# One block for all stages of a two-layer hybrid kernel, and one normalisation in the place of two

## What is computed

```
for stage in (selective scan, mixture, multi-query attention, mixture,
              grouped-query attention, capacity mixture, windowed attention, capacity mixture):
    x = x + stage(layernorm(x))        # layernorm: (x - mean) / sqrt(var + 1e-5)
```

```
xn = layernorm(x)
mu = jnp.mean(xn); var = jnp.var(xn)
xn = (xn - mu) * rsqrt(var + EPS) * gamma
```

## Time and profile before

| | us |
|---|---|
| median of 3 runs | 1926.79 (1923.84 to 1929.45) |
| the profiled execution | 1924.93 |
| its span, first to last instruction | 1923.1 |
| mean granted TensorE clock | 0.944 of full speed |

### The profile page before, as it was taken

The page is one execution under the profiler, slowest core; times in us unless marked ns, Lnnn a source line. Parts: engine busy times, 40 slices in busy tenths (PEclk is TensorE's granted clock), DMA queues, the critical chain, the costliest instruction groups (busy, mean ns, idle before and its releaser), DMA issues. The chain is left out here.

```text
span 1923.1 us, 35959 instructions
## 1 busy us (share of the span) xinstructions
PE 1702.3 (89%) x10911; PEld 1365.3 (71%) x10912; DVE 1355.2 (70%) x2857; ACT 1002.8 (52%) x2208; POOL 664.6 (35%) x640
## 2 busy tenths in 40 slices
PE   3877999599999899979999997987799999988986
PEld 1224888477777788857777796765688888887764
DVE  7997666878885566678777748554888888657643
ACT  4654443477874344357777633111687887633111
POOL 1663222266662022236656503000455555212000
PEclk8997999799999899989999997999899999988988
DMA  0000110100000011010000003696211000021984
GB/s 29 0 1 27 45 48 28 53 20 19 19 8 1 23 50 49 27 55 23 25 19 14 1 1 120 202 252 178 75 31 30 25 30 11 1 84 55 262 239 134
DMA packets 39478, 111.15 MB, mean 58 GB/s; under 512 B 5504, under 2 KB 23664, under 8 KB 32240
## 3 DMA queue, kind: packets, MB, share of 16 engines
q1 hardware_dynamic: 39408, 110.26, 19.8%
HBM read 109.19 MB, written 1.05 MB: 57 GB/s over the span
## 5 line engine op out<-in xcount | busy, mean ns | idle before, releaser
L1320 POOL TENSOR_TENSOR xn<-xn 128x512 f32<-128x512 f32 x138 | 180.2, 1306 | 272.0 <-DVE xn L1215 272.0
L1306 POOL TENSOR_SCALAR prob<-prob,recip 128x256 f32<-128x256 f32 (+2 forms) x256 | 229.8, 912 | 71.6 <-DVE recip L1199 71.5
L1110 ACT ACTIVATE prob<-banks,peak 128x256 f32<-128x256 f32 (+3 forms) x384 | 190.4, 501 | 104.1 <-DVE peak L1190 97.9
L959 PE MATMUL banks<-pt,v 128*128 128x256 f32 (+3 forms) x768 | 204.4, 409 | 6.9 <-ACT pt L1045 6.9
L959 PEld LDWEIGHTS banks<-pt,v 128*128 128x128 f32 x768 | 145.2, 190 | 73.9 <-issue 31.9
L914 PE MATMUL banks<-k_hi,q_hi 128*128 128x256 f32 (+2 forms) x384 | 154.2, 401 | 25.1 <-DVE k_lo L1206 24.8
L1190 DVE TENSOR_REDUCE peak<-banks 128x1 f32<-128x256 f32 (+3 forms) x384 | 161.6, 448 | 20.5 <-PE banks L918 17.6
L594 POOL TENSOR_TENSOR gu_lo<-gu,gu_hi 128x512 fp32r<-128x512 f32 x36 | 46.8, 1301 | 294.6 <-ACT gu_hi L552 294.6
L935 PE MATMUL banks<-ident,prob 128*128 128x128 f32 x864 | 142.5, 282 | 3.2 <-DVE pt L1043 3.2
L563 ACT ACTIVATE silu<-gate 128x512 f32<-128x512 f32 x72 | 43.1, 599 | 159.1 <-PE up L515 159.0
L1215 DVE TENSOR_TENSOR xn<-xn,ropes 128x512 f32<-128x512 f32 x138 | 124.3, 901 | 0.0
(11 more groups left out here) (249 smaller groups left out, 5193.3 us busy)
## 6 DMA issues: line engine op xcount, KB each, us to landing
wgu<-in_w_gu SPq DMA_DIRECT2D x32, 1408.0 KB, 14.8
wd<-in_w_d SPq DMA_DIRECT2D x32, 704.0 KB
gu<-in_w SPq DMA_DIRECT2D x36, 256.0 KB, 2.7
wd<-in_w SPq DMA_DIRECT2D x36, 128.0 KB, 2.0
wkv<-in_mha_kv SPq DMA_DIRECT2D x16, 256.0 KB, 2.6
wq<-in_mqa_q SPq DMA_DIRECT2D x16, 128.0 KB, 2.0
wo<-in_mqa_o SPq DMA_DIRECT2D x16, 128.0 KB, 2.2
wq<-in_gqa_q SPq DMA_DIRECT2D x16, 128.0 KB, 2.1
```

The costliest lines, as they stand in the source:

```text
L959: last = pe.matmul(o_bank[:, x * P:to], v[:, s, x, at:at + P], pt[:, s, x, first:first + to - x * P], start=(j == 0), stop=(j == NQ - 1))
L1110: last = act.activation(prob[:, s, cols[t]:cols[t] + n], s_bank[gi][:, psum_col[t]:psum_col[t] + n], ACT.Exp, bias=peak[:, s, t:t + 1], ac ...
L1306: last = pool.tensor_scalar(part, part, recip[:, s, t:t + 1], None, ALU.mult)
L1320: pool.tensor_tensor(cosed[:, r % 2, :], cosed[:, r % 2, :], swap[:, r % 2, :], ALU.add) \
```

## The change

All stages come to stand in one block; the barriers, and the separate blocks at the start and the end, go. A stage becomes an object that holds a body for each engine, and each engine's program in the one block runs the bodies one after the other. SBUF is cut into four fixed zones (0 to 64, 64 to 96, 96 to 142 KB, and the rest) in place of allocation per stage, and every tile is put into a zone such that what the next stage loads early does not overlap what is still in use. PSUM is one tensor of 8 banks, used by each stage as before.

The links between stages are these. VectorE's statistics of tile pair j wait for the addition to that pair, by a count that the additions raise:

```
-        for r in range(self.rounds):
-            src = g.xn if r else g.x
-            for h in range(2):
...
+        for t in range(NT):
+            if t % 2 == 0 and self.after:
+                count, first = self.after
+                wait(dve, count, first + t // 2 + 1)
+            dve.bn_stats(g.bn[:, t, :], g.x[:, t, :]).then_inc(self.stats.sem, 1)
```

```
+            if self.again:
+                op = act.activation(g.std[:, cut], g.mv[:, cut, 1], ACT.Sqrt, scale=1.0 + EPS, bias=g.eps2[:, 0:1])
+            else:
+                op = act.activation(g.std[:, cut], g.mv[:, cut, 1], ACT.Sqrt, bias=g.eps[:, 0:1])
```

with eps2 = EPS * EPS: normalising twice divides by sqrt(var + EPS) * sqrt(var / (var + EPS) + EPS), which is sqrt(var * (1 + EPS) + EPS * EPS). The store is cut into four in the last stage:

```
+        if out is not None:
+            for t in range(0, NT, 2):
+                sp.wait_ge(c["added"].sem, t // 2 + 1)
+                sp.dma_start(out[:, t:t + 2, :], g.x[:, t:t + 2, :]).then_inc(c["stored"].sem, 16)
+            sp.wait_ge(c["stored"].sem, 16 * NT // 2)
```

More of the change, by code:

```diff
@@ L1 @@
-from contextlib import ExitStack
+import math
 import concourse.bass as bass
@@ L438, in selective_scan @@
-    finish(nc, [*c.values(), *norm.counts])
-def mixture(nc, g, d):
-    c = {n: Count(nc, n, p) for n, p in (
+    _, _, early, _ = st.areas()
+    late = Area(st.nc, g.zones[0][0], g.zones[1][1])
+    xw = late.take("xw", [P, NC, XROWS], F32)
+    dtw = late.take("dtw", [XROWS, H], F32)
+    vecs = late.take("vecs", [P, 2 * NC + NC * N_STATE], F32)
+    pick1 = late.take("pick1", [A3, HALF], F32)
+    pick = late.take("pick", [A3, HALF, P], BF16)
+    rows = late.take("rows", [XROWS, T], F32)
@@ new lines, in selective_scan @@
+    rest = early.take("rest", [A3, T], F32)
+    part = early.take("part", [A3, T], BF16)
+    stack = late.take("stack", [A3, T], BF16)
+    nega = late.take("nega", [P, NC, N_STATE], F32)
+    size = early.take("size", [P, NC, T], F32)
+    e = early.take("e", [P, NC, T], F32)
+    lg = early.take("lg", [P, NC, T], F32)
+    relu = early.take("relu", [P, NC, T], F32)
+    lost = early.take("lost", [P, NC, T], F32)
+    delta = late.take("delta", [P, NC, T], F32)
+    du = late.take("du", [P, NC, T], F32)
@@ L448, in mixture @@
+def mixture(st, g, d, free, after):
+    c = st.c = {n: st.count(n, p) for n, p in (
         ("loaded", 0), ("gu_even", 0), ("gu_odd", 0), ("d_even", 0), ("d_odd", 0), ("logits", 0), ("gates", 0),
@@ L695, in attention @@
+def attention(st, g, d, after, name, kv_every, window, gamma=None, again=False):
     UNITS = HEADS * NSEQ
@@ new lines, in out_half @@
+        def out_half(u):
+            t, half = u // 2, u % 2
+            wait(pe, c["wo_low"], HEADS)
+            wait(pe, c["o_low"], u + 1)
+            to = banks[:, t // 2, (t % 2) * H:(t % 2 + 1) * H]
+            for h in range(WO):
+                o_hi, o_lo = (part[:, half, h, :] for part in o_stage)
+                hi, lo = (w[:, half * WO + h, :] for w in (wo_hi, wo_lo))
+                pe.matmul(to, o_hi, hi, start=(half == h == 0), stop=False)
+                pe.matmul(to, o_hi, lo, start=False, stop=False)
+                last = pe.matmul(to, o_lo, hi, start=False, stop=(half == 1 and h == WO - 1))
+            last.then_inc(c["o_used"].sem, 1)
@@ L1359, in capacity_mixture @@
+def capacity_mixture(st, g, d, free, after, opened, out=None):
+    c = st.c = {n: st.count(n, p) for n, p in (
         ("loaded", 0), ("own_v", 0), ("logits", 0), ("shared_w", 0), ("peak", 0), ("expd", 0), ("masked", 0),
@@ L1876, in stages @@
-def stages(nc, g, ins):
-    selective_scan(nc, g, ins)
-    mixture(nc, g, ins)
-    attention(nc, g, ins, "mqa", kv_every=HEADS, window=False, gamma=g.gamma, again=True)
-    mixture(nc, g, ins)
-    attention(nc, g, ins, "gqa", kv_every=4, window=False)
-    capacity_mixture(nc, g, ins)
-    attention(nc, g, ins, "mha", kv_every=1, window=True)
-    capacity_mixture(nc, g, ins)
+    low, high = -(-nc.sbuf_base // 64) * 64, nc.sbuf_usable_end // 32 * 32
+    kept = Area(nc, low, high)
+    g.x = kept.take("x", [P, NT, H], F32)
```

2905 lines of the change are left out of this document (1476 added, 1429 removed).

## The result

The new kernel takes 1896.91 us (median of four runs, 1892.51 to 1902.75) where the kernel before took 1927.11 in the same comparison: a ratio of 0.9846, 95% interval 0.9812 to 0.988. The new kernel is 30 us faster; 11.8 were forecast, and 1896.9 lies outside the range of 1904 to 1921.5. The profiled execution took 1892.51 (span 1890.7) against 1924.93 (span 1923.1): 32.4 us of span to find.

A forecast was written before the change was run, and what follows sets the result against it. TensorE, busy 89% of the span, bounds the kernel; its standing time can be won. 7.0 + 6.1 + 3.1 + 2.1 + 2.5 - 9.0 = 11.8 us off, so 1915.0 us median, range 1904 to 1921.5.

The forecast's parts named there:

- The term of the shared weights: Earlier loads in capacity mixtures: 2.5 us off in the normalisations, 9.0 us on in the two output projections before them.
- The second normalisation: Start of the multi-query attention: one normalisation round instead of two, 6.1 us off, bounds 5.9 and 6.3.
- The start: Kernel start: earlier loads let GpSimd's cast of `pick` finish sooner, freeing the first scaling; 3.1 us off, bounds 0.7 and 3.4.
- the estimate of 7.0 to 10.6 for the cast: Kernel start: when GpSimd's cast of `pick` would run in the new kernel, instead of 10.10 to 13.69.
- The end: Kernel end: four stores of 256 KB following the additions instead of one of 1 MB; 2.1 us off, bounds 1.4 and 2.5.
- The barriers: Stage changes: VectorE goes from last addition to next statistics without the barrier gap; 7.0 us off, bounds 6.5 and 8.6.
- the 1.6 us for VectorE's semaphore increments: Stage changes: increments ahead of the normalisation, 0.09 us each, expected to stay and taken from the 8.6 us of gaps.
- the rule cited from the Trainium skill: VectorE contends with GpSimd only with two SBUF inputs or in a two-port mode; by it the sum is 11.8, otherwise 9.4.
- The wait of TensorE: Output projections before the capacity mixtures: GpSimd's long subtraction holds VectorE's `xl`, so TensorE loses 3.2 us in each.
- The 1.3 us for a drop of the clock: Same output projections: a low-clock drop after TensorE's pause, added per stage to the wait, making 4.5 us.
- Rival (b): Expert loops: new slot places lengthen TensorE's waiting for weights by a quarter, 6 us go, time 1921.0; chance 0.13.

The follow-up runs named there:

- experiment 3: Kernel before with its stage tiles moved up by 32 bytes and one normalisation in the multi-query attention: median 1906.1 us, ratio 0.9835 to the kernel before.
- Experiment 8: New kernel with nearly all expert weight transfers left out (14 of 16 groups load only 8 of 128 partitions): 1869.3 us, runs 5.5 us apart.
- the second comparison: New kernel unchanged, run once more against the kernel before: median 1893.1 us against 1921.1, ratio 0.9879 (0.9829 to 0.993).

## Why the prediction was wrong

Two steps failed. The term of the shared weights (2.5 off, 9.0 on, so 6.5 on) measured 3.2 off and 5.1 on, so 1.9 on. And everything that the change does not move was costed at nothing, the heads of the attentions and the expert loops above all, and came out 17 us shorter in the profiled pair.

**Which steps held.** The second normalisation: 6.16 us, 6.1 forecast. The start: 0.86 + 2.30 = 3.2, 3.1 forecast, and the estimate of 7.0 to 10.6 for the cast was 6.95 to 10.54. The end: 1.8, 2.1 forecast: the last store needed 3.0 us, not 2.7. The barriers: 8.6, 7.0 forecast; the 1.6 us for VectorE's semaphore increments ahead of a normalisation do not show up. And the rule cited from the Trainium skill (SBUF — State Buffer, Who interferes with whom) holds by the rows at 6.11 and 7.71: statistics beside GpSimd's cast take 1.40 and 1.37 us.

**The shared weights.** In the two profiles the normalisations give 1.56 and 1.66 (from the first statistics to the shared expert's first matmul, 15.86 to 14.30 and 15.61 to 13.95), 3.2 in all; the projections cost 2.56 each, 5.1. The wait of TensorE was right (2.90 for 3.2). Two parts of the term failed. The 1.3 us for a drop of the clock came in neither projection of this profile. That was not a rule: ten projections of five profiles have such a pause of 2.9 us, and in two of them a drop of 3.4 us follows it (the new kernel moved up by 32 bytes, first projection, at 1104.1; the one without reloads, second, at 1649.8), and these two took 2.0 and 1.7 us longer than the same projections of the new kernel. And the unspoken assumption that the projection's own pace stays: with the wait taken off, it gained 0.3 us, and 1.0 in the projection of the multi-query attention, which has no such wait. With the forecast's terms replaced by what they measured the sum is 8.6 + 6.2 + 3.2 + 1.8 + 3.2 - 5.1 = 17.9 instead of 11.8. Without the end and the normalisation it is 9.9, and experiment 3 has 9.4 for the block.

**What no step spoke of.** Two things that are not moved were not nothing:

- The heads of the attentions, 8.5 us, and the first output projection, 1.0. One part is the pace: 0.16 us in each two-head iteration of the multi-query attention, at most 1.5 us in the grouped-query one, where the drops of the clock are as many as before, and 0.15 in an iteration of the windowed one with a drop (37.4 us instead of 37.56); some 3.5 us in all, an estimate. The other part is the clock. In the multi-query attention the first two heads take 1.3 us less, with the low clock ending 3.4 instead of 4.8 us behind the first projection matmul, and the last two 1.8 less, with a drop at their end gone. The windowed attention has a pause of TensorE of 1.7 to 1.9 us in each iteration. TensorE's timeline and a window (last figures: granted clock, DMA share, GB/s) before:

```profile
1405.75 0.38 PE L914 MATMUL banks<-k_hi,q_hi 128*128 128x256 f32 x1 [1.82 <-DVE k_lo L1206]
```

```profile
1408.00:1409.00 1.00, 1.00 (x7) 0.50 0.00 0
```

and after:

```profile
1418.35 0.39 PE L959 MATMUL banks<-k_hi,q_hi 128*128 128x256 f32 x1 [1.86 <-DVE k_lo L1252]
```

```profile
1420.00:1421.00 1.00, 1.00 (x11) 1.00 0.00 0
```

The same pause, once with a drop to 1.2 GHz behind it and once without. From 1405 us on, the kernel before has the drop in 7 of 7 iterations, 37.55 us each; the second profile of it repeats 37.56. The new kernel has it in 4 of 7 (in its second profile in 5), and an iteration without it takes 36.65. The Trainium skill (TensorE: Matmul & The Clock Gate, Part 1: The HAM clock gate) says that the cost of the gate varies from run to run with the phase of its own observation; the rows agree that the pause alone does not decide. Where two iterations in a row have a drop, the drops are 37.5 to 37.6 us apart in every profile, which is the length of the old iteration; so the old loop may have been in step with the drops. That is a guess: no run changed the length alone. What is shown is that both profiles of the unchanged kernel have all seven drops, and that with tiles shifted by 32 or 64 bytes it has four and one.

- The expert loops, 7.5 us in the profiled pair. Rival (b) took up only that the change might slow them, and the sum used the length they had in one execution. Ten loops of the old structure take 139 to 154 us and sixteen of the new, with all transfers, 136 to 153. Their sums are 295 and 288 us on average; whether the change has a part in this difference stays open, since single sums go from 278 to 304. Experiment 8 shows that the transfers make this spread.

So 17.9 us are the forecast's own steps at their measured prices. Some 5 us are the places of the tiles and the drops of the clock; they are read from profiles and not shown in the times. What is left of the 30 is within what the loops do by chance. Outside the loops the change brings 1625.6 - 1604.5 = 21.1 us and 1.8 at the end, 22.9, in line with the 23 us of the second comparison's ratio. The bounds of the forecast's terms ended at 24.4 and held this, but by luck: 5 of the 22.9 us belong to no term. The range ended at 1904, 22.8 below the median, and had nothing for the spread of the loops, because the three runs shown lay within 5.6 us.

## What to carry to other kernels

Cut two profiles at the same instructions and compare stretches before looking for a cause: a stretch that has the same instructions and another length is a transfer rate, a clock or an address, and a second profile of the unchanged kernel tells which of it repeats. A stretch that waits for transfers belongs in the range with its own spread, which three runs need not show. Of a fused block the gain at a boundary is the chain of the engine that ends one stage and begins the next; moving that chain into its earlier pauses gave more (11.8 us at three boundaries) than removing the barriers (8.6 at seven), and long GpSimd instructions beside VectorE's two-input ones cost less in pieces.

## What was unexpected of the hardware

An unused tile of 32 bytes per partition made the attentions' matmuls faster: half-tiles of 24 matmuls 2.81 us apart on average instead of 2.85, two-head iterations 27.64 instead of 27.81; 64 bytes gave 2.84 and 27.70. Which operand does it was not tried. The drops of the clock repeat in two profiles of the unchanged kernel, in the attentions to 0.1 us of their place in the stage, and move when the tiles are shifted. Everything outside the transfer-bound loops took the same time in sum, to 0.04 us, in these two profiles. Keeping TensorE busy through a pause of 5.8 us kept the clock up only until the sparse transposes behind it in two of three attentions, and in none of them did it save time.
